# Where the derived token quarters of a two-level product come from: TensorE transposes, or GpSimd sums of quarters that are already turned

## What is computed

```python
xn = layernorm(x)
s  = attention(xn)                      # 16 heads, relative bias, layer norm with gamma, beta
h  = square(relu(xn @ W_fc.T))          # 512 -> 2048
y  = h @ W_proj.T                       # 2048 -> 512
g  = silu(spikes(y) / 5)                # five steps of a recurrence with a threshold
out = x + s * g
```

## Time and profile before

| | |
|---|---|
| median of 3 runs | 3512.62 us |
| profiled execution | 3514.12 us, of which the span is 3512.3 us |
| feed-forward stage | about the first 1370 us of the span |
| TensorE busy | 3382.1 us, 96% |
| VectorE, ScalarE, GpSimd busy | 2805.5 us (80%), 2778.6 us (79%), 1862.4 us (53%) |
| granted TensorE clock, mean | 0.997 |

### The profile page before, as it was taken

How to read it: one execution, slowest core, us unless ns; L and a number is a source line. 1 busy time by engine, 2 the same in 40 slices (tenths; PEclk the granted TensorE clock), 3 DMA queues, 4 the chain that set the end, 5 groups by cost and what they waited for, 6 DMA issues and landing times.

```text
span 3512.3 us, 63651 instructions
## 1 busy us (share of the span) xinstructions
PE 3382.1 (96%) x22764; PEld 1691.8 (48%) x22764; DVE 2805.5 (80%) x4814; ACT 2778.6 (79%) x4529; POOL 1862.4 (53%) x1094
## 2 busy tenths in 40 slices
PE   6999999999999999999999999999999999999996
PEld 4666666666666665334334333433433433433431
DVE  7878877777877866777788788788888888888877
ACT  6555444444444446999999999999999999999997
POOL 4222333223222314898766766766766666666662
PEclk9999999999999999999999999999999999999999
DMA  5655655555555543222332232232322322322322
GB/s 203 212 165 176 192 179 176 188 190 175 173 175 169 172 151 121 70 67 81 114 98 80 90 94 81 92 94 80 94 90 82 95 85 85 97 85 82 100 61 85
DMA packets 257226, 430.34 MB, mean 123 GB/s; under 512 B 98672, under 2 KB 134256, under 8 KB 256912
## 3 DMA queue, kind: packets, MB, share of 16 engines
q1 hardware_dynamic: 231088, 294.13, 27.1%
q10 hardware_dynamic: 25824, 132.13, 10.9%
HBM read 284.75 MB, written 83.95 MB: 105 GB/s over the span
## 4 chain that ended last, share of the span: by engine, by line
ACT 33%; PE 12%; issue 10%; DVE 4%; SPq 1%; DMA 1%; ACTq 0%; POOL 0%; DVEq 0%; POOLq 0%
ACT recurrence_or_probs L1906 17%; ACT s_sb L1913 16%; PE misc L1780 3%; PE s_ps L1835 3%; PE s_ps L1821 3%; PE acc L1855 3%; DVE s_sb L1977 2%; DMA xT<-xnT 1%; SPq L320 1%; PE misc L1762 0%; DVE gate_or_tokens L2106 0%; DVE outT L1997 0%; DVE x_or_queries L2014 0%; DVE gate_or_tokens L2109 0%; PE s_ps L1780 0%
## 5 line engine op out<-in xcount | busy, mean ns | idle before, releaser
L1977 DVE TENSOR_SCALAR_CACHE_REDUCE s_sb<-s_ps 128x1024 f32<-128x1024 f32 x998 | 1214.5, 1221 | 352.9 <-PE s_ps L1821 324.7
L2183 POOL TENSOR_TENSOR recurrence_or_probs<-recurrence_or_probs,toep 128x512 f32<-128x512 f32 (+1 forms) x375 | 1289.1, 3458 | 362.1 <-ACT recurrence_or_probs L1906 356.2
L1913 ACT ACTIVATE s_sb<-s_sb,nmax 128x1024 f32<-128x1024 f32 x998 | 1166.4, 1169 | 9.6 <-DVE s_sb L1977 9.3
L1906 ACT ACTIVATE recurrence_or_probs<-s_ps 128x1024 f32<-128x1024 f32 x1024 | 1060.6, 1037 | 8.1 <-PE s_ps L1835 7.8
L744 PE MATMUL ps_y<-w_pr,hid_part 128*128 128x512 f16 x3072 | 808.6, 379 | 0.0
L1855 PE MATMUL acc<-recurrence_or_probs,val 128*32 128x512 f32 x4096 | 545.1, 604 | 2.3 <-DVE recurrence_or_probs L2093 1.5
L982 ACT ACTIVATE snap<-ps_fc 128x256 f32<-128x256 f32 x384 | 147.5, 384 | 470.6 <-PE ps_fc L727 455.6
L123 POOL TENSOR_TENSOR recurrence_or_probs<-gate_or_tokens,gamma_beta 128x512 f32<-128x512 f32 x60 | 86.0, 1434 | 597.3 <-DVE gate_or_tokens L178 596.2
L744 PEld LDWEIGHTS ps_y<-w_pr,hid_part 128*128 128x128 f16 x3072 | 300.6, 98 | 173.8 <-issue 0.3
L727 PE MATMUL ps_fc<-xnT_part,w_fc 128*128 128x256 f16 x2304 | 315.5, 273 | 17.9 <-DVE u L1335 11.7
L1821 PE MATMUL s_ps<-kst,qst 96*128 96x512 f16 x1024 | 306.0, 380 | 24.0 <-ACT recurrence_or_probs L1906 23.9
(11 more groups left out here) (200 smaller groups left out, 4083.3 us busy)
## 6 DMA issues: line engine op xcount, KB each, us to landing
w_fc<-fc_made ACTq DMA_DIRECT2D x120, 896.0 KB, 5.1
toep<-table_rows SPq DMA_DIRECT2D x32, 2048.0 KB, 8.2
x_or_queries<-x_or_queries SPq DMA_DIRECT2D x384, 64.0 KB, 2.0
xnT<-xnT_part SPq DMA_DIRECT2D x32, 512.0 KB, 11.3
x_or_gate<-in_x SPq DMA_DIRECT2D x16, 1024.0 KB, 9.0
base<-x_or_gate SPq DMA_DIRECT2D x16, 1024.0 KB, 7.6
xT<-xnT SPq DMA_DIRECT2D x32, 512.0 KB, 9.6
result<-gate_or_tokens SPq DMA_DIRECT2D x64, 256.0 KB, 2.1
```

Source lines behind the costliest of these rows:

```text
L1906: nc.scalar.activation(prob[:, k % PROBS, 2 * second:2 * second + 2, :].rearrange("p j n -> p (j n)"), s_ps[:, item_buffer(pair_item(m)), ...
L1913: nc.scalar.activation(s_sb[:, i % 4, :], s_sb[:, i % 4, :], ACT.Exp, bias=nmax[:, par, j, st:st + 1], scale=-1.0, accum_out=den[:, par, j ...
L1977: nc.vector.tensor_scalar(s_sb[:, i % 4, :], s_ps[:, item_buffer(tile_item(n)), :], -1.0, None, ALU.mult, ALU.min, accum_out=nmax[:, par, ...
L2183: nc.gpsimd.tensor_tensor(tile, tile, toep[:, par, :, at:at + width], ALU.add).then_inc(biased, 1)
```

## The change

BY_TENSOR is 2: chunks 1 and 2 keep the old way. For chunk c + 1 from 3 to 15 (made during chunks 2 to 14, 13 times):

- No transposes of derived quarters on TensorE, and no copies from PSUM on ScalarE. The natural tokens alone are split and turned by the same 32 DMAs, now sorted by quarter, with a semaphore for each of the four quarters, and sent only when all eight halves are there.
- GpSimd joins each turned natural quarter (high + low half, f16 to f32, into the buffer of xn) as it lands and makes the four sums from those: eight instructions in place of four, between and ahead of its twelve gate instructions.
- ScalarE and VectorE split the sums straight into `xnS`: high halves in pairs 5, 6, 6 and 7, low halves in pairs 6, 6, 6 and 7.
- Everything ahead of that comes one pair earlier: statistics in pair 7 of chunk c - 1, normalising in pair 0, both halves of x in pair 1 (four low halves in that step).
- x of chunk c + 2 is loaded by SyncE, ahead of the transposes of c + 1, since the buffer of x is free once the tokens are normalised.
- The last chunk's gate order stays, that of chunks 2 to 14 becomes one tile in each of pairs 4, 5, 6 and 7. The low halves of w_q, w_k, w_v (pairs n = 23, 30, 31) are spread over their step.

```diff
-TURN_AT = {c * 8 + 5 + (c == 0) + h: (c + 1, 2 * h) for c in range(15) for h in range(2)}
+TURN_AT = {6: (1, 0), 7: (1, 2), 13: (2, 0), 14: (2, 2)}
-GATES_AT = ({4: (0,), 5: (1,), 6: (2,)}, {4: (0,), 6: (1, 2)})
+GATES_AT = ({4: (0,), 5: (1,), 6: (2,)}, {4: (0,), 6: (1, 2)}, {4: (0,), 5: (1,), 6: (2,)})
+        def prepared(n, k):
+            n -= k
+            if n == 1:
+                return 1
+            if n == PAIRS:
+                return 2
+            c = (n + 1) // PAIRS + 1
+            return c if n > PAIRS and n % PAIRS == PAIRS - 1 and c < NC else None
+        def natural(par, part, q):
+            k, half = ((2, HALF), (0, 0), (0, HALF), (2, 0))[q]
+            return xnT[:, par, part, k:k + 2, half:half + HALF]
...
+                def block(part, t, k):
+                    sp.dma_start(xnT[:, par, part, k, t * P:(t + 1) * P], xn_part[:, part, t, k * P:(k + 1) * P],
+                                 transpose=True).then_inc(xt_turned[((1, 3), (2, 0))[t // 2][k // 2]], 16)
...
+                else:
+                    sp.wait_ge(xn_hi, c * 4)
+                    sp.wait_ge(xn_lo, c * 4)
+                    for t, k in ((2, 0), (2, 2), (0, 0), (0, 2)):
+                        for part in range(2):
+                            for i in range(4):
+                                block(part, t + i // 2, k + i % 2)
...
+                if BY_TENSOR <= c < NC - 2:
+                    sp.wait_ge(xn_ready, c * 4 + 8)
+                    load_x(c + 2)
                 if c < NC - 1:
                     turn(c + 1, 1 - par)
+                if c + 1 == BY_TENSOR:
+                    sp.wait_ge(turn_lo, BY_TENSOR * 4)
+                    load_x(BY_TENSOR + 1)
...
+            def join_quarter(c, q, done):
+                if done == 0:
+                    pool.wait_ge(xn_hi, c * 4)
+                    pool.wait_ge(xn_lo, c * 4)
+                pool.wait_ge(xt_turned[q], c * TURNED)
+                nc.gpsimd.tensor_tensor(xn[:, q, :].rearrange("p (k s) -> p k s", k=2), natural(c % 2, 0, q), natural(c % 2, 1, q),
+                                        ALU.add).then_inc(sum_made, 1)
+            def turned_sum(c, q, a, b, op, done):
+                pool.wait_ge(sum_made, (c - 1 - BY_TENSOR) * 8 + done)
+                nc.gpsimd.tensor_tensor(xn[:, q, :], xn[:, a, :], xn[:, b, :], op).then_inc(sum_made, 1)
...
+            for c in range(BY_TENSOR, NC - 1):
+                join_quarter(c + 1, 2, 0)
+                join_quarter(c + 1, 0, 1)
+                turned_sum(c + 1, 0, 0, 2, ALU.subtract, 2)
+                spiking.multiply(c - 1, 0)
+                join_quarter(c + 1, 1, 3)
+                turned_sum(c + 1, 2, 2, 1, ALU.subtract, 4)
+                turned_sum(c + 1, 1, 0, 1, ALU.add, 5)
+                join_quarter(c + 1, 3, 6)
+                turned_sum(c + 1, 3, 3, 1, ALU.subtract, 7)
+                for t in range(1, 4):
+                    spiking.multiply(c - 1, t)
...
+                if c > BY_TENSOR and p == 0 and i in (2, 3, 4, 6):
+                    made = (c - 1) * 4 + {2: 2, 3: 2, 4: 3, 6: 4}[i]
+                    pe.wait_ge(turn_hi, made)
+                    pe.wait_ge(turn_lo, made)
...
+                    act.wait_ge(sum_made, (c - 1 - BY_TENSOR) * 8 + (3, 6, 6, 8)[j])
+                    nc.scalar.activation(xnS[c % 2][:, 0, j].rearrange("p k s -> p (k s)"), xn[:, j, :], ACT.Copy).then_inc(turn_hi, 1)
...
+                    hi, lo = (xnS[c % 2][:, part, j].rearrange("p k s -> p (k s)") for part in range(2))
+                    nc.vector.tensor_tensor(lo, xn[:, j, :], hi, ALU.subtract).then_inc(turn_lo, 1)
```

More of the change, by code:

```diff
@@ L409, in feed_forward @@
         turn_lo = sem("turn_lo")
-        xt_turned = sem("xt_turned")
+        xt_turned = [sem(f"xt_turned{q}") for q in range(4)]
+        sum_made = sem("sum_made")
         xs_copied = sem("xs_copied")
@@ L608, in _ @@
                 sum_quarters(p)
[L609 to L615, removed]
+            for c in range(1, BY_TENSOR):
+                make_turns(c + 1)
                 for t in range(4):
                     spiking.multiply(c - 1, t)
-                    if c == NC - 1 and t == 0:
-                        first.subtracted(pool, 0, 0, 0)
+            for c in range(BY_TENSOR, NC - 1):
[10 more added lines that the diff above has]
+                    spiking.multiply(c - 1, t)
+            wait_turned(pool, NC - 1)
+            nc.gpsimd.memset(first.kst[ROWS:ROWS + SUBTRACTED], 1.0).then_inc(first.ones_set, 1)
+            pool.wait_ge(first.ones_set, 1)
+            for t in range(4):
+                spiking.multiply(NC - 2, t)
+                if t == 0:
+                    first.subtracted(pool, 0, 0, 0)
         @block.tensor
@@ L1346, in step @@
                 c, p = n // PAIRS, n % PAIRS
-                ahead, late = c < NC - 1, c == 0
+                ahead = c < NC - 1
+                begun, refined, split = prepared(n, 0), prepared(n, 1), (prepared(n, 2), prepared(n, 3))
+                whole = split[0] if split[0] and split[0] > BY_TENSOR else None
+                split = [part if part and part <= BY_TENSOR else None for part in split]
+                summing = BY_TENSOR <= c < NC - 1
                 square(2 * n - 1)
                 first_max(n - 1, 3)
-                if ahead and p == 0 + late:
-                    statistics(c + 1, 0)
+                if begun:
+                    statistics(begun, 0)
                 count(n, 0)
-                if ahead and p == 3 + late:
-                    part_lo(c + 1, 2)
+                if split[1]:
+                    part_lo(split[1], 2)
                 if c and p == 7:
@@ L1362, in step @@
                     projection_lo(2 * n - 1)
[L1363 to L1376 removed]
+                if n in QKV_LO_AT:
+                    qkv_lo(QKV_LO_AT[n], 0)
+                if whole:
+                    part_lo(whole, 0)
+                if summing and p == 6:
+                    turned_lo(c + 1, 0)
+                if begun:
+                    for t in range(1, 4):
+                        statistics(begun, t)
+                if refined:
+                    refine(refined)
+                    normalise(refined, 0)
+                    normalise(refined, 1)
+                count(n, 1)
+                if split[0]:
+                    part_lo(split[0], 0)
+                if whole:
+                    part_lo(whole, 1)
+                if split[1]:
+                    part_lo(split[1], 3)
+                if c and p in GATES_AT[ahead * min(c, 2)]:
+                    for t in GATES_AT[ahead * min(c, 2)][p]:
                         spiking.gate_tile(c - 1, t)
@@ L1379, in step @@
                 if n in QKV_LO_AT:
-                    for k in range(3):
-                        qkv_lo(QKV_LO_AT[n], k)
+                    qkv_lo(QKV_LO_AT[n], 1)
                 hid_lo(2 * n - 1)
                 first_max(n, 1)
+                if n in QKV_LO_AT:
+                    qkv_lo(QKV_LO_AT[n], 2)
                 if n < PAIRS - 1:
                     quarters_lo(n + 1, 0)
-                if ahead and p == 1 + late:
-                    normalise(c + 1, 2)
+                if refined:
+                    normalise(refined, 2)
+                if whole:
+                    part_lo(whole, 2)
+                if summing and p in (6, 7):
+                    turned_lo(c + 1, 1 if p == 6 else 3)
                 count(n, 3)
                 combine(n, 1)
-                if ahead and p == 0 + late:
-                    variances(c + 1)
+                if begun:
+                    variances(begun)
                 if n < PAIRS - 1:
@@ L1394, in step @@
                         quarters_lo(n + 1, m)
-                if ahead and p == 1 + late:
-                    normalise(c + 1, 3)
+                if refined:
+                    normalise(refined, 3)
                 count(n, 4)
-                if ahead and p == 2 + late:
-                    part_lo(c + 1, 1)
-                if ahead and p in TURNS_LO_AT[c > 0]:
-                    for j in TURNS_LO_AT[c > 0][p]:
+                if split[0]:
+                    part_lo(split[0], 1)
+                if whole:
+                    part_lo(whole, 3)
+                if c < BY_TENSOR and p in TURNS_LO_AT[c]:
+                    for j in TURNS_LO_AT[c][p]:
                         turned_lo(c + 1, j)
+                if summing and p == 6:
+                    turned_lo(c + 1, 2)
                 if n in QKV_LO_AT:
```

111 lines of the change are left out of this document (56 added, 55 removed).

## The result

The changed kernel takes **3550.62 us**, the median of 4 runs (3542.86 to 3553.91), beside 3512.89 us for the kernel before on the same chip (4 runs, 3511.75 to 3513.84): a ratio of 1.0103 [1.0091, 1.0116]. It is slower by 1%, where the prediction said 3503. The profiled execution is the fastest of the four: 3542.86 us with a span of 3541.1, which is 28.8 more than the span before.

A forecast was written before the change was run, and what follows sets the result against it. TensorE was taken as the bound, busy 79.19 of 80 us. Transposes -23.4, new stalls +11.7 and once-costs +2 summed to -9.7 us, giving 3503 us against a median of 3512.62; the range was 3479 to 3532.

The forecast's parts named there:

- Transposes removed, 23.4 us: TensorE's path, chunks 3 to 15: 4 x 0.45 = 1.80 us a chunk, 13 times, 23.4 us gained.
- One held instruction of VectorE for each back-to-back instruction of GpSimd: VectorE under GpSimd's bursts: one SBUF instruction per GpSimd instruction, 1.68 us instead of 0.61, 1.07 us paid each.
- The 4.3 us a chunk that a hold would have cost: VectorE, pair 7: estimated extra if the four one-input statistics were also held by GpSimd, about 4 x 1.07 us.
- Join 1.6 us: GpSimd: length assumed for one join with f16 inputs, from 1.27 us undisturbed and 1.60 against VectorE.
- Pair 7, 1.6 us: Fourth burst fills pair 7: second combine comes at some 10.1 us, product 6 wants it by 8.45, 1.6 us late.
- The landing: Transposed quarters, with 3 us (between 0 and 6) for x ahead: at 34, 45, 56 and 67.5 us into a chunk.
- the working gives 2.0 us: New stall a chunk: 0.4 us around pairs 4 and 5 plus 1.6 in pair 7, where 1.13 stood.
- the second rival: Bursts land on combines, first in pair 4, if x is through early: stall 5 to 7 us; 3542 at 5; chance 0.22.
- The once-costs, 2 us: Paid once: 1 us for chunk 1's load of x, 1 us for low halves of w_q at n = 23.
- The 1 us for the load of x in chunk 1: SyncE loads x of chunk 3 behind chunk 1's transposes: 0 to 4 us, taken 1.
- The rival that GpSimd costs nothing in pair 7: VectorE keeps up: fourth burst costs TensorE nothing, second misses the combine, stall 0.4 us, 3482 us; chance 0.2.
- the ring of queues: SyncE, DMA, GpSimd: 75.5 to 78 us; with x's 3 us, beat 80 to 81, 3512 to 4 us more; chance 0.13.

The follow-up runs named there:

- experiment 2: Changed kernel with GpSimd's joins and sums narrowed to 16 of 512 columns, all waits kept: 3504.31 us, 0.9977 of the kernel before.
- Experiment 6: Experiment 5 with the low half of the last sum moved from pair 7 to pair 0 of the next chunk: 3501.46 us, 0.9962 of the kernel before.
- Experiment 5: experiment 1 with the low halves of w_q, w_k, w_v moved to pairs 0 to 3 of chunk 3: 3512.26 us, 0.9996 of the kernel before.
- experiment 1: Changed kernel with SyncE holding the transposes until product 0 of pair 2, 2.3 us later: 3522.09 us, 1.0033 of the kernel before.
- experiment 7: Experiment 6 with the transposes held another 2.6 us, until product 2 of pair 2: 3505.84 us, 0.9973 of the kernel before.
- experiment 3: Kernel before with only one of eight transposes of a derived quarter for chunks 3 to 15: 3493.69 us, 0.9946 of the kernel before.

## Why the prediction was wrong

**Transposes removed, 23.4 us: right.** 19 to 20 us measured for 7/8 of them.

**One held instruction of VectorE for each back-to-back instruction of GpSimd: right.** 1.75 us at 912.51, 915.39, 917.07. (Each ends some 0.5 us behind a GpSimd instruction, though, and not with it: 912.51 + 1.75 = 914.26, the sum ahead of it 912.12 + 1.60 = 913.72.) The statistics were the doubt. Chunk 7, pair 7, where GpSimd runs without a gap from 688.68 to 706.36:

```profile
696.63 1.60 POOL L123 TENSOR_TENSOR recurrence_or_probs<-gate_or_tokens,gamma_beta 128x512 f32<-128x512 f32 x1
...
697.03 1.87 DVE L1303 BATCH_NORM_STATS2 stats<-x_or_queries 128x6 f32<-128x512 f32 x3
698.82 1.32 DVE L1409 TENSOR_TENSOR hid_part<-hid,hid_part 128x512 f16<-128x512 f32 x1
700.05 1.75 DVE L1363 TENSOR_TENSOR xnS_part<-x_or_queries,xnS_part 128x512 f16<-128x512 f32 x1
701.73 0.41 DVE L1417 TENSOR_TENSOR u<-ps_fc,snap 128x256 f32<-128x256 f32 x1
```

Three of them take 1.87 us together, 0.62 each: they run beside GpSimd, unheld, while the two-input instructions behind them take 1.32 and 1.75. By that the rule of the Trainium skill (SBUF — State Buffer, section SBUF: two separate sides), that an instruction of VectorE with one SBUF input and outside the two-port modes takes no part in the lock, agrees with the trace. The 4.3 us a chunk that a hold would have cost were not paid.

**Join 1.6 us: a little high.** 1.24 mean of 52, 1.15 at the least: two f16 inputs took 1.15 us where two f32 inputs took 1.27. By the Trainium skill (GPSIMD Engine Reference, sections 1 and 2.1) approximately 2.5 cycles an element, at 1.2 GHz, are the floor of a two-input instruction, by estimate 1.07 us for 512 elements. The trace agrees in so far as neither of the two times is below it.

**Pair 7, 1.6 us: right, in part by luck.** 1.5 on the mean of ten chunks, and experiment 2 shows that it is the gate burst with the low half of the last sum, as the working had it. Experiment 6 takes it away. But two of its terms were off and balance: in chunk 7 the five held instructions take 1.26, 1.16, 1.42, 1.32 and 1.75 us, 6.9 together where the sum had 8.4, and the four statistics 2.55 where it had half of 2.7.

**The landing: here it failed.** The step is "Taking 3, the quarters land at ... 45": the bounds were 0 and 6 us for the 1 MB of x ahead of the transposes, and one value between them was taken for all chunks. But x costs the second quarter little, although it is not through when the transposes start. It goes out 7.5 to 13.3 us into each of the ten chunks and lands at 20 to 27, with the transposes from 18.2 on; in chunk 10, where it goes out at 877.08, by SyncE's load alone:

```profile
DMA to landing us min/median/max: 13.5/13.5/13.5
```

In chunk 9 it lands last of all, at 27.2, and the second join comes at 40.4. What keeps a second quarter back is another queue's weight load at 40.0 us, which it meets or escapes by 2 us at the most. Two outcomes, 41 and 45, stood in place of the one value. In those chunks where the landing is 45 the working gives 2.0 us against 2.9 measured; where it is 41 the second rival gives 5 to 7 against 7.0. The rival's place and price came true in six chunks of ten, but its condition ("If x is through early") in none, so its reason was not the right one. And 45 came true in four by the weight load, not by the 3 us for x: that is luck. Between the forecast's -9.7 us and the measured +28.8 lie 38.5; this step makes 6 x (7.0 - 2.0) = 30 of them, the falls of the clock in chunks 11 and 12 included. The range ended at 3532, below the 3542 that the prediction itself gave for this rival.

**The once-costs, 2 us: too small.** Chunks 2 and 3 took 8.5 us more than before, where the sum had 2 x (-0.9) and 1 for the low halves of w_q: 9 us more than that. The working named n = 23 alone; n = 30 and 31 carry the low halves of w_k and w_v into pairs 6 and 7 of chunk 3, under the same burst, and were not priced. Experiment 5 gives 10 us back by moving them all. (The 1 us for the load of x in chunk 1 was not paid: that chunk takes 81.06 us, 80.99 before.)

**The clock: not thought of.** It falls once each in chunks 2, 3 and 11 and twice in chunk 12; the fall in chunk 11 cost 1.7 us.

**The rival that GpSimd costs nothing in pair 7** falls by the 1.5 us there, and **the ring of queues** by SyncE's rows in chunk 10, where x goes out 10 us before the transposes, which wait for the low halves alone (18.2 us in every chunk), and by experiments 1 and 7:

```profile
877.08 0.38 SPq L509 DMA_DIRECT2D x_or_queries<-in_x  x1
887.74 43.43 SPq L516 DMA_TRANSPOSE xnT_part<-x_or_queries  x32
```

**What stays open.** What decides, chunk by chunk, how many hold-ups the first fifteen transposes meet; why chunk 3 is late; at which idle times the clock falls; the rest of pair 5's stall in experiment 6. The runs of the changed kernel differ by 11 us among themselves, those of the kernel before by 2: at 4 us for each chunk that changes its kind this would be some three chunks, but only one run was profiled, so this is argued and not shown.

## What to carry to other kernels

Where a burst on GpSimd is released by a transfer, its place among VectorE's instructions is as uncertain as the landing: price both ends of that landing by the chunk, and if they lie on either side of a combine, tie the start to the engine that suffers, with a wait, as experiment 1 did for 28 us. Work that was removed from the bounding engine brought its full price here (experiment 3), and the bursts that replace it must be laid, instruction by instruction, against the other engine's queue in the few chunks with extra work too. What would be held there is best moved to where the other engine rests (experiments 5 and 6: 20 us).

## What was not expected of the hardware

A DMA transpose issued 0.5 us ahead of another queue's 896 KB load landed in 5.5 us, one issued 1.1 us ahead of it in 2.4. And TensorE's granted clock fell to 0.50, for some 3 us, behind idle times of 2.07 us (chunk 11), 2.10 and 2.08 us (chunk 12), in stretches where TensorE was otherwise busy, while idle times of 2.32 us (pair 6 of chunk 10) and 2.27 us (pair 6 of chunks 5, 9 and 13) left it at 1.00. So the length of the idle time alone does not tell whether it falls; what else does is open. In chunk 11 a stall of 2.2 us cost 1.7 on top.
